# Attention, latent attention and experts on one core: the small tasks of all five engines take other places between the score units

## What is computed

```python
xn = layernorm(x)
out = x + attn(xn) + ffn(xn)          # two branches, both read xn
# attn: 16 heads of 8, causal softmax(q k^T / sqrt(8)) v, then Wm
# ffn:  x2 = xn + latent_attention(rmsnorm(xn)) Wo   # 16 heads: 32 plain + 32 rotary channels,
#                                                    # keys and values from a latent of 16
#       out_ffn = x2 + moe(rmsnorm(x2))
# moe:  8 experts of width 64, best 2 by softmax(x Wgate + bias), and one shared expert
```

## Time and profile before

| | |
|---|---|
| median of 3 runs (lowest, highest) | 1433.71 us (1433.46, 1439.99) |
| the profiled execution's own time | 1436.47 us |
| its span | 1434.6 us |
| TensorE busy | 93% |
| VectorE, ScalarE, GpSimd busy | 79%, 59%, 49% |
| mean granted TensorE clock | 0.95 |
| two blocks (a pair), steady | 81.0 to 82 us |

### The profile page before, as it was taken

The page is one execution under the profiler, slowest core; times in us unless marked ns, Lnnn a source line. Parts: engine busy times, 40 slices in busy tenths (PEclk is TensorE's granted clock), DMA queues, the critical chain, the costliest instruction groups (busy, mean ns, idle before and its releaser), DMA issues.

```text
span 1434.6 us, 40077 instructions
## 1 busy us (share of the span) xinstructions
PE 1332.3 (93%) x16484; PEld 938.6 (65%) x16484; DVE 1133.0 (79%) x2298; ACT 850.4 (59%) x1329; POOL 709.3 (49%) x800
## 2 busy tenths in 40 slices
PE   4698899999999999999999999999999999999986
PEld 3465666666776666666666667667667666666554
DVE  7767697979889796978979798887979788787623
ACT  1045566666666665666666666656666665666572
POOL 4443445566454555645455565545556554554112
PEclk8579999999999999999999999999999999999998
DMA  7745555543554454354555534554543454454100
GB/s 191 151 99 110 113 116 119 125 117 74 123 127 116 113 136 107 76 120 113 126 116 127 122 85 114 123 118 111 134 117 92 91 131 111 114 132 109 26 2 15
DMA packets 139993, 156.43 MB, mean 109 GB/s; under 512 B 32896, under 2 KB 126756, under 8 KB 133668
## 3 DMA queue, kind: packets, MB, share of 16 engines
q1 hardware_dynamic: 139812, 153.87, 46.0%
HBM read 83.10 MB, written 67.11 MB: 105 GB/s over the span
## 4 chain that ended last, share of the span: by engine, by line
PE 63%; DVE 25%; issue 8%; ACT 2%; SPq 0%; POOL 0%; DMA 0%; DVEq 0%; POOLq 0%
PE ps L226 22%; PE psm L226 15%; PE pse L226 11%; DVE R L767 10%; PE psv L226 8%; PE ps L353 2%; DVE rt L838 2%; DVE tc_ L731 1%; PE ps L419 1%; DVE xs L707 1%; DVE ts_ L733 1%; DVE ts_ L732 1%; DVE vA L740 1%; DVE pB L722 1%; DVE kt_ L754 1%
## 5 line engine op out<-in xcount | busy, mean ns | idle before, releaser
L767 DVE TRANSPOSE_TENSOR_REDUCE R<-psm 128x32 f32<-128x1024 f32 x384 | 478.4, 1246 | 196.4 <-PE psm L226 194.2
L1144 ACT ACTIVATE PT<-pse 128x1024 f32<-128x1024 f32 x384 | 393.6, 1025 | 322.5 <-PE pse L226 322.4
L226 PE MATMUL pse<-qsB,ks 128*128 128x512 f32 (+1 forms) x768 | 217.1, 418 | 2.0 <-ACT pse L1148 1.3
L1296 POOL TENSOR_TENSOR sm<-sm,half 128x2 f32<-128x2 f32 x32 | 23.0, 718 | 342.4 <-DVE sm L682 342.4
L226 PE MATMUL psm<-qsB,ksm 128*128 128x256 f32 (+1 forms) x640 | 141.4, 337 | 37.9 <-DVE R L767 28.5
L1148 ACT ACTIVATE pse<-maskb 128x512 f32<-128x512 bf16 x256 | 143.4, 592 | 4.1
L226 PEld LDWEIGHTS psm<-qsB,ksm 128*128 128x128 f32 x640 | 96.1, 196 | 69.8 <-DVE R L767 51.6
L1158 ACT ACTIVATE OT<-psv 128x512 f32<-128x512 f32 x128 | 76.2, 595 | 83.8 <-PE psv L226 83.8
L226 PEld LDWEIGHTS pse<-qsB,ks 128*128 128x128 f32 (+1 forms) x768 | 104.0, 193 | 33.2 <-ACT pse L1148 14.3
L226 PE MATMUL psv<-PT,vA 128*9 128x128 f32 x3072 | 101.8, 279 | 13.6 <-issue 11.8
L1332 POOL TENSOR_TENSOR tc_<-tc_,ts_ 128x512 f32<-128x512 f32 x64 | 81.9, 1280 | 64.7 <-DVE ts_ L733 64.7
(11 more groups left out here) (196 smaller groups left out, 2794.6 us busy)
## 6 DMA issues: line engine op xcount, KB each, us to landing
scrB<-pB SPq DMA_DIRECT2D x64, 768.0 KB, 5.6
qsB<-scrB SPq DMA_DIRECT2D x128, 384.0 KB
scrA<-pA SPq DMA_DIRECT2D x128, 96.0 KB, 2.3
qsA<-scrA SPq DMA_DIRECT2D x128, 64.0 KB
ksA<-scrA SPq DMA_DIRECT2D x128, 64.0 KB
xs<-in_x SPq DMA_DIRECT2D x16, 256.0 KB, 2.8
qsA<-scrA SPq DMA_DIRECT2D x128, 32.0 KB
ksA<-scrA SPq DMA_DIRECT2D x128, 32.0 KB
```

Source lines behind the costliest of these rows:

```text
L226: return e.matmul(o, l, r, start=start, stop=stop, skip_group_check=True)
L767: e.tensor_reduce(red, MX[:].rearrange("p i (c q) -> p (i c) q", q=32), AX.X, ALU.max, apply_transpose=True).then_inc(s_mr, 1)
L1144: e.activation(PT[g % 4], EX[:], ACT.Exp, scale=(8.0 ** -0.5, 0.125)[br]).then_inc(s_pt, 1)
L1296: e.tensor_tensor(sm[:, 1, c], sm[:, 0, c], half[:, 0:2], ALU.pow).then_inc(s_pw1, 1)
```

## The change

No operation is added or removed, and no tile. The lists of small tasks of PE, DVE, ACT, POOL and SP are written in another order. The core of the diff, with what the text speaks of:

```diff
@@ PE, ahead of the units @@
-                    if k == 0:
-                        if even and done:
-                            moe_d(p - 1, (4, 0))
+                    if k == 0 and even and done:
+                        moe_d(p - 1, (4, 0))
+                    if k == 1:
                         if soon:
                             prep_x(n2)
+                        if before:
+                            pv_half(1, c - 1, 1)
...
-                    if k == 3:
-                        if even and done:
-                            moe_t(p - 1)
-                        if before:
-                            tail_out(c - 1)
+                    if k == 3 and odd and moe:
+                        moe_g(p, 4)
...
+                    if k == 9:
+                        if even and moe:
+                            moe_g(p, 0)
+                        if odd and moe:
+                            moe_sel(p, 2)
@@ PE, behind the units @@
+                    if k == 6 and body:
+                        pv_half(0, c, 1)
...
+                        if even and moe:
+                            moe_g(p, 1)
                     if k == 11 and even and moe:
-                        moe_g(p, 1)
                         moe_u(p, 1)
@@ DVE @@
+                    if k == 4:
+                        if n1 < NB:
+                            prep_k2(n1)
+                        if soon:
+                            prep_a1(n2)
...
+                    if k == 9:
+                        if odd and moe:
+                            moe_hu(p, 2)
+                        if even and moe:
+                            moe_route1(p)
+                            moe_route2(p)
                     if k == 10:
                         if even and moe:
+                            moe_route3(p)
                             moe_hg(p, 0)
...
-                        if even and moe:
-                            moe_route2(p)
-                            moe_route3(p)
@@ POOL @@
+                    if k == 7:
+                        if n1 < NB:
+                            prep_km(n1, 1)
                         if soon:
-                            prep_rope(n2, 0)
+                            prep_kt(n2)
+                            prep_rope(n2, 0)
+                    if k == 8:
+                        if even and moe:
+                            moe_split(p)
                         if soon3:
                             stats2(n2 + 1)
+                    if k == 9:
                         if soon:
-                            prep_rope(n2, 1)
+                            prep_rope(n2, 1)
+                        if soon3:
+                            prep_n(n2 + 1)
...
+                    if k == 11 and soon:
                         prep_rlo(n2)
@@ SP @@
-                    if k == 3 and soon:
+                    if k == 6 and n1 < NB:
+                        max_row(0, n1)
+                    if k == 7 and soon:
                         stack_a(n2)
...
+                    if k == 9 and soon:
+                        stacks_b(n2)
+                    if k == 11 and n1 < NB:
+                        max_row(1, n1)
```

More of the change, by code:

```diff
@@ L611, in _ @@
                             join_max(1, c)
[L612 to L613 removed]
+                        if before:
+                            norm(1, c - 1, 1)
                     if k == 2:
@@ L1021, in _ @@
[L1021 to L1028, removed]
+                    if k == 1 and soon:
+                        prep_xlo(n2)
+                    if k == 4:
+                        if n1 < NB:
+                            prep_k2(n1)
+                        if soon:
+                            prep_a1(n2)
@@ L1061, in _ @@
                             setup_rest()
+                    if k == 0:
+                        if odd and moe:
+                            moe_hu(p, 1)
+                        if body:
+                            join_max(1, c)
                     if k == 1:
@@ L1099, in _ @@
                             moe_hu(p, 3)
-                        if even and moe:
-                            moe_route4(p)
                         if body:
@@ L1225, in _ @@
                     br, u = divmod(k, 6)
-                    if k == 0:
-                        if odd and moe:
-                            moe_th(p, 1)
-                        if soon:
-                            prep_x(n2)
+                    if k == 0 and even and done:
+                        moe_sel(p - 1, 3)
+                    if k == 1 and before:
+                        evict(1, c - 1, 1)
                     if k == 2:
+                        if even and done:
+                            moe_d(p - 1)
@@ L1258, in _ @@
-                    if k == 1 and even and done:
-                        moe_d(p - 1)
-                    if k == 2:
                         if soon:
@@ L1403, in _ @@
                 for k in range(12):
-                    if k == 0:
+                    if k == 0 and even and done:
+                        moe_h(p - 1, 2)
+                    if k == 1 and even and done:
+                        moe_h(p - 1, 3)
+                    if k == 2 and soon:
+                        prep_r0(n2)
+                    if k == 3:
                         if soon3:
@@ L1408, in _ @@
                             prep_ks(n1)
+                    if k == 4 and soon:
+                        prep_r1(n2)
+                    if k == 5:
+                        if n1 < NB:
                             prep_km(n1, 0)
-                    if k == 1:
-                        if soon:
-                            prep_r0(n2)
-                            prep_r1(n2)
+                        if before:
+                            tail(c - 1)
+                    if k == 6:
+                        if even and moe:
+                            moe_x(p)
+                        if odd and moe:
+                            moe_h(p, 0)
+                            moe_h(p, 1)
```

226 lines of the change are left out of this document (92 added, 134 removed).

## The result

The changed kernel takes 1394.97 us (median of 4 runs, 1393.29 to 1399.95), the kernel before 1436.85 (4 runs, 1433.46 to 1448.59): the ratio is 0.970, with a 95% interval of 0.964 to 0.977. It is 42 us faster; the prediction was 1448, in a range of 1406 to 1478. A later batch gave 0.972 (0.967 to 0.977) for the same two kernels.

The account below looks back on a forecast made before the run. TensorE, busy 93% of the span, was taken as the bound: only its waits, low-clock stretches and array-division changes count. Terms summed to +0.9 us a pair, +14 over some 15 pairs: 1450, as run median 1448; range 1406 to 1478.

Parts of the forecast that it names:

- The stands at units 8, 9 and 11 go, and the mask's wait at unit 9: -1.5: Even c: TensorE's waits at units 8, 9 and 11 and for ScalarE's mask vanish, 1.5 us less a pair.
- 1.5 to 1.7 lost for each fall: Around unit 9 of the even c: us lost when the clock drops to 0.50, about once a pair.
- Rival (a): The clock's fall at unit 9 goes, 1.6 us a pair over 15 pairs: 1423 us; chance 0.15.
- Rival (c): The clock's fall goes and the added waits are half as large, both together: 1403 us; chance 0.12.
- a pair under 81.0: Sign of a wrong prediction: a pair of blocks taking less than 81.0 us, against 81.5 in the pair read before.
- +0.65: Two small VectorE instructions ahead of max unit 4 delay it: +0.45 us in the odd c, +0.2 in the even.
- +0.3: VectorE's odd slots at units 1, 3 and 6 come out 0.3 us later net, between 0 and 0.8.
- The stand for `x2lo`: Even c, ahead of unit 9: TensorE's `moe_g(p, 0)` waits for GpSimd's `x2lo`, a new stand of 0.75 us.
- The short slot behind unit 11 and the masks: Even c: too little TensorE work behind unit 11, +0.48 us; mask waits at units 10 to 11 and 5 to 6, +0.35.
- Route 3 beside `prep_n`: Even c, from 10.5 us after unit 7's start: VectorE's route 3 meets no wait there and takes 1.35 us.
- rival (d): Route 3 waits for `pB`, perhaps `xn` and `h`: about 2.1 us a pair more, 1479 us; chance 0.13.
- SP: hidden: Stack transfers start some 6 us later for the first attention, some 3 for the others, without costing time.

Follow-up runs that it names:

- Experiment 5: Kernel before, with GpSimd's low-row rounding moved to the end of slot 11, waiting for VectorE's norm, and row transfers one slot later: 1409.46 us, ratio 0.984.
- experiment 1: Changed kernel, with GpSimd's low-row rounding moved from slot 11 to slot 9, back beside the route: 1398.99 us, ratio 0.971.
- h4: Changed kernel, with SP's list of DMA issues taken from the kernel before: 1397.13 us, ratio 0.970.
- experiment 4: Whole engine lists mixed between the kernel before and the changed one, four mixtures: 1537.17, 1491.91, 1533.62 and (h4) 1397.13 us.
- f1: The kernel of Experiment 5: kernel before, GpSimd's low-row rounding made to wait for VectorE's norm of slot 10: 1409.46 us, ratio 0.984.

## Why the prediction was wrong

**The step that failed: "The stands at units 8, 9 and 11 go, and the mask's wait at unit 9: -1.5".** That these waits go was right; the size was that of one pair. At unit 11 it counted 0.6, from the earlier trace rows; without the fall in unit 9 the stand measures 2.26 (the pair at 424 us), and the term is 0.28 + 0.29 + 2.26 + 0.3 = 3.1. Experiment 5 takes the cause that the prediction names for this stand out of the old kernel and gains 23 us, where 0.6 a pair would be 9. The sign of the sum hung on it: with -3.1 in its place, +0.9 becomes -0.7 a pair, 1423. That is still inside the range; the rest of the miss is in the terms below that didn't come.

**The clock was entered as a cost beside the stands.** I had estimated 1.5 to 1.7 lost for each fall and taken it as staying. In the old kernel a fall in unit 9 cost nothing up to unit 11, for the 10.9 of VectorE's chain held the pair in either case; a fall behind the stand did cost 1.5. So stand and fall have no separate prices: where the new kernel has a fall at the start of unit 9, slots 7 to 11 take 19.7, 0.5 less than before, which is about the 0.5 of transposes that moved out of them, and the prediction's own terms for these slots sum to -0.1; where it has none they take 18.2. Rival (a), that the fall goes, was worked out as independent of the stands, at 0.15. It is not independent: with the job moved away (experiment 5) 10 of 14 pairs are without a fall there, where none was before. Rival (c) came closest, 1403, by a sum of two halves for the wrong reason. Of the signs named for being wrong, a pair under 81.0 came: 79.1.

**Terms that didn't come.** "+0.65" for `prep_k2` and `prep_a1` ahead of max unit 4: slots of 1.89 in both parities, as before. In the odd c the two small instructions do stand there (773.43 to 773.94) and the reduction ends at 775.18, 0.2 ahead of the next unit: TensorE's slot 3, which holds the tasks that came from the slots beside it, is 1.2 longer (4.13 instead of 2.91), so that VectorE came into slot 4 0.5 to 0.6 earlier. I had moved VectorE's tasks and left TensorE's old slots under them. "+0.3" for the odd slots: they fall by 0.8, from 39.25 to 38.45; 0.31 of it is the stand of the earlier trace rows, some 0.3 the mask's waits at unit 8, the rest is several small ones. The even units 0 to 6 take 0.5 more (22.4 after 21.9): that is `prep_x`, whose transposes (0.52, at 445.14 in the pair shown) stood in slot 11 and now stand behind unit 0.

**Terms that came.** The stand for `x2lo`: +0.75 predicted, 0.95 measured. The short slot behind unit 11 and the masks: +0.83 predicted; 0.30 stand and 0.46 of mask waits measured. Route 3 beside `prep_n`: no wait, with its steps at 0.15 to 0.33. `pB` behind it, not in it: rival (d) did not come, and by experiment 1 its wait of 1.6 would have cost next to nothing there, not 2.1 a pair. L842 took 1.33, not 0.6, in a place where it is free. SP: hidden, as h4 shows. The array's division: 0.1, not seen in the total.

With the measured terms the sum closes. Units 7 to 11 of the even c: -3.1 - 0.2 + 0.95 + 0.76, and -0.5 for the transposes that left, is -2.1 (20.3 to 18.2). With the rest, -0.8 + 0.5, it is -2.4 a pair, the difference between the shortest pairs of each kernel (81.4 and 79.1, to 0.1). Over fifteen pairs that is 36 us, what lies between the two profiled spans. It is not a full account, for most pairs are longer than the shortest: the mean of slots 7 to 11 is 1.0 above it before and 1.2 in the changed kernel, so by this profile the falls there give nothing of the gain beyond this sum.

**What stays open.** Of the 42 us experiment 5 accounts for 23. Part of the other 19 are its three long pairs, by its shortest pair 1.9 of 2.3 us are there; the rest lies in other orders of all five lists at once and could not be taken apart in time, since partial sets of lists don't fit together (experiment 4). Whether a stand brings on a fall is seen only as a count over pairs, which varies for one kernel (9 and 5) as much as between some of them; no run held the stand and changed nothing else.

## What to carry to other kernels

Look at several periods before sizing a stand: if neighbouring periods reach the same point after the same time by two patterns, the engine whose interval is the same in both (here VectorE, 10.9 us) sets the pace, and the stand is as large as in the pattern where nothing else is slow. When tasks of all engines move, rebuild every engine's slots before placing one list against another's old times; a late task costs only what is left after the other engine's own wait. And a place in the list of an idle engine doesn't say when an instruction runs: to keep it away from something, make it wait for what must come first.

## What the runs showed of the hardware

- A VectorE instruction of 32 elements took 1.82 to 2.31 us beside GpSimd's 128x1024 subtraction and 1.33 beside its 128x512 addition, always ending within 0.1 us of it; beside GpSimd's TENSOR_SCALAR of 128x128 the steps took 0.15 to 0.33. The Trainium skill (SBUF — State Buffer, "Who interferes with whom") has a VectorE instruction with two SBUF inputs contend with a GpSimd instruction that reads SBUF. The rows beside the subtraction and the addition agree; by those beside TENSOR_SCALAR it was at most 0.14 us (0.33 against 0.19).
- The granted clock falls to the lower level (0.50, that of 1.2 GHz). Ahead of the falls read here TensorE had done the gate product with its 8 columns, or stood. Mean granted clock over the runs: 0.951 before (0.945 to 0.954 in 11 runs), 0.960 in the changed kernel, 0.961 in f1 (0.959 to 0.967). What a fall costs by the slots is 1.5 us, in the changed kernel up to 2.2 where it comes in ahead of unit 9, and 0 where VectorE's chain hides it.
- The profiles have stands of 1 to 4 us in the midst of a stream of equal products, with nothing that released them; they lie elsewhere in each kernel (in f1 three of 3.5 to 3.9 us, at 412, 820 and 1228, with the clock low beside them). What they are was not tested.
